# Attention stage of a graph kernel: scores ahead of the keys, and queries between the two gate products, in TensorE's order

## The reference

```python
q = (node_attr @ Wq).reshape(n, H, DQ // H)
x_src = node_attr[src]
# for keys and for values, each with its own weights:
#   rad = relu(edge_attr @ W1 + b1) @ W2 ; g = edge_sh @ Wang.T
#   conv = x_src * g @ Wlin * rad
alpha = jnp.einsum('ehq,qk,ehk->eh', q[dst], Wdot, k)
amax = jax.ops.segment_max(alpha, dst, num_segments=n)
ealpha = jnp.exp(alpha - amax[dst])
denom = jax.ops.segment_sum(ealpha, dst, num_segments=n)
out = jax.ops.segment_sum((ealpha / denom[dst])[..., None] * v, dst, num_segments=n) @ Wout
```

## Time and profile before

| | |
|---|---|
| median of 3 timed runs | 4299.57 us (4296.43 to 4299.69) |
| span of the profiled execution | 5039.6 us |
| TensorE matmuls busy | 4108.6 us, 82% |
| VectorE busy | 3024.4 us, 60% |
| ScalarE busy | 1972.1 us, 39% |
| GpSimd busy | 1919.0 us, 38% |

### The profile page before, as it was taken

The page is one execution under the profiler, slowest core; times in us unless marked ns, Lnnn a source line. Parts: engine busy times, 40 slices in busy tenths (PEclk is TensorE's granted clock), DMA queues, the critical chain, the costliest instruction groups (busy, mean ns, idle before and its releaser), DMA issues. The chain is left out here.

```text
span 5039.6 us, 74127 instructions
## 1 busy us (share of the span) xinstructions
PE 4108.6 (82%) x26543; PEld 3350.2 (66%) x26543; DVE 3024.4 (60%) x4129; ACT 1972.1 (39%) x2885; POOL 1919.0 (38%) x2002
## 2 busy tenths in 40 slices
PE   4667999999999984688888888888888888888832
PEld 4656999999999973465665666666666566666622
DVE  8985544544444342566666666666666666666734
ACT  5754666655665531222222223222223222222313
POOL 5640000000000015555555555555555555555352
PEclk9878999999999985799989999999999999999965
DMA  7998999999998533455555665556666655566433
GB/s 169 188 188 263 298 295 297 294 295 297 292 292 267 182 101 94 133 163 163 164 156 152 166 163 161 162 165 166 164 163 164 166 164 157 159 164 164 141 114 47
DMA packets 1012838, 944.08 MB, mean 187 GB/s; under 512 B 705677, under 2 KB 811929, under 8 KB 1012339
## 3 DMA queue, kind: packets, MB, share of 16 engines
q1 hardware_dynamic: 952099, 814.71, 55.7%
q0 software_dynamic: 60368, 124.52, 11.1%
HBM read 648.66 MB, written 289.97 MB: 186 GB/s over the span
## 5 line engine op out<-in xcount | busy, mean ns | idle before, releaser
L2313 POOL DMA_INDIRECT feats_hops<-x_table,src_s x1616 | 1546.9, 957 | 1223.1 <-PE e_turn_ps L2423 771.8
L1286 PE MATMUL acc<-t_wide,scaled 128*128 128x448 f32 x6860 | 1409.0, 366 | 24.2 <-DVE t_wide L1380 24.2
L1286 PEld LDWEIGHTS acc<-t_wide,scaled 128*128 128x128 f32 x6860 | 1284.3, 188 | 129.2 <-DVE scaled L1398 24.6
L1321 ACT CAST t_wide<-t_ring 128x1568 fp32r<-128x1568 uint8 x490 | 737.7, 1506 | 564.9 <-PE acc L1286 543.8
L1380 DVE CAST t_wide<-t_ring 128x1568 fp32r<-128x1568 uint8 x490 | 478.3, 976 | 733.4 <-PE acc L1286 714.9
L2484 ACT COPY e_out_rows<-e_turn_ps 128x512 f32<-128x512 f32 x404 | 222.1, 588 | 1026.5 <-remote 932.5
L1809 POOL MEMSET l_eps<- 128x1 f32 x1 | 0.1, 104 | 1452.9 <-POOLq L1498 1452.9
L2423 PE MATMUL e_turn_ps<-ident,feats_hops 128*128 128x128 f32 x1616 | 250.3, 296 | 355.6 <-ACT e_out_rows L2484 292.4
L2401 PE MATMUL e_ring_ps<-e_wlin_v,e_x_gv 128*128 128x128 f32 x3232 | 432.7, 281 | 96.9 <-issue 85.6
L2401 PEld LDWEIGHTS e_ring_ps<-e_wlin_v,e_x_gv 128*128 128x128 f32 x3232 | 393.0, 194 | 115.9 <-issue 102.2
L2569 DVE TENSOR_TENSOR e_lw<-e_ring_ps,e_w_t 128x1024 f32<-128x1024 f32 x202 | 247.1, 1223 | 366.9 <-remote 249.6
(11 more groups left out here) (272 smaller groups left out, 5096.2 us busy)
## 6 DMA issues: line engine op xcount, KB each, us to landing
t_ring<-adjacency_bytes SPq DMA_DIRECT2D x490, 512.0 KB, 5.8
sums_table<-e_out_rows SPq DMA_DIRECT2D x202, 576.0 KB
q_first<-hop_zeros_q SPq DMA_DIRECT2D x101, 512.0 KB, 5.9
e_sh<-parts_sh SPq DMA_DIRECT2D x404, 128.0 KB
e_ea<-parts_ea SPq DMA_DIRECT2D x404, 128.0 KB
e_q_rows<-q_first SPq DMA_DIRECT2D x404, 128.0 KB
e_same<-same_row SPq DMA_DIRECT2D x404, 128.0 KB
adjacency_bytes<-lists_staged SPq DMA_DIRECT2D x196, 256.0 KB
```

The source lines that it names most:

```text
L1286: mm = nc.tensor.matmul(acc[c][:, 0:n], U[p][:, b, :], wide[m % WIDE_RING][:, lo:lo + n], start=(b == 0 and p == 0), stop=(b == NB - 1 and ...
L1321: nc.scalar.copy(into, of).then_inc(wide_act, 1)
L2313: nc.gpsimd.indirect_dma_start(x_rows[i % XR][:, g * GT + t, :], None, x1_table, bass.IndirectOffsetOnAxis(ap=src_ix[:, at:at + 1], axis=0 ...
```

## The change

In each turn, TensorE does the scores of the preceding pair in front of `keys_and_radial`, no longer behind it, and the transposes of the queries between gate 0 and gate 1, no longer behind gate 1. Everything else stays.

```diff
@@ -2461,15 +2461,15 @@
                     radial_values(i, j)
                 if chain_at(i - 2) is not None:
                     turn_weights(chain_at(i - 2), i)
+                if on(i - 1):
+                    scores(i - 1)
                 if on(i):
                     keys_and_radial(i)
-                if on(i - 1):
-                    scores(i - 1)
                 if on(i + 1):
                     hidden(i + 1, i)
                     gates(i + 1, 0, p_gk)
+                    turn_q(i + 1)
                     gates(i + 1, 1, p_gv)
-                    turn_q(i + 1)
                 if on(j):
                     spread_out(j, i)
```

## The result

The changed kernel takes 4320.01 us (median of 4 runs, 4319.65 to 4322.35) against 4299.63; the ratio is 1.0048, 95% interval 1.0036 to 1.0061, so 15 to 26 us slower. Five more runs in later rounds gave 4320.91 us, 1.0050 (1.0036 to 1.0063). Forecast were 4327, slower.

The account below looks back on a forecast made before the run. TensorE was taken to set the attention stage's turn. 255 more shape switches at 0.17 us add 43 us, waits won take off 16: +27, put at 4327 us; range 4284 to 4358, the forecast's own 4312 to 4343.

Parts of the forecast that it names:

- The stall: Attention stage: ScalarE's unnamed waits before copying out sums belong to the profiled execution alone, making its missing 740 us.
- TensorE sets the turn: Attention stage: TensorE sets the pace at 10.4 us a turn, ahead of GpSimd's 10.1 and VectorE's 9.4.
- The price of a switch: TensorE's order: each change of array shape costs 0.17 us (0.13 to 0.22); 255 more of them, 43 us.
- The wait won: Second gate's wait for VectorE's key product, every fourth turn: 0.49 less 0.17 before the values, 16 us in 50 groups.
- The sum: Whole kernel: 43 us of switches less 16 us of waits won, +27 us, put at 4327.
- The cheap switches: Rival on TensorE's order: switches below 0.06 us, so the kernel is faster, 4284 or 4275 us; chance 0.17.
- GpSimd as the pace: Rival: GpSimd's 10.1 us or the unnamed stall sets the turn, so time stays the same, 4300 us; chance 0.15.
- no wait is won: Rival at the second gate: no wait goes, so slower still, 4343 to 4365 us; chance 0.1.

Follow-up runs that it names:

- more_switches: Kernel before with scores moved between the hidden matmuls and the gates, and queries between the two gates: 4341.51 us, ratio 1.0098.
- b0_again: The kernel before, unchanged, run once more with a profile: 4297.73 us, ratio 0.9998, profiled span 4296.0.
- scores_between: Kernel before with scores moved between the radial key matmul and the keys, and queries between the gates: 4289.65 us, ratio 0.9979.
- scores_only: Kernel before with only the scores moved in front of the radial key matmul, queries left behind the second gate: 4344.51 us, ratio 1.0104.
- queries_only: Kernel before with only the queries moved between the two gates, scores left behind the keys: 4277.81 us, ratio 0.9949; again 4276.33, 0.9946.
- fewer_switches: Kernel before with order keys, scores, radial key, queries between the gates, and VectorE's two products swapping operands: 4280.03 us, ratio 0.9952.

## Why the prediction was right

*The stall.* Taken for a thing of the one execution because its size was that of the missing 740 us: shown, by a second execution without it. What caused it stays open. That all 740 us lay in the attention stage was not so: 710 did, and the stage has 2133 us without it, where the prediction had 2103.

*TensorE sets the turn.* Right: in `more_switches` two more switches lengthen every kind of turn by 0.31 to 0.37 us (medians, against the queries alone), and TensorE is busy 98% of the stage. But the agreement on which the prediction rested, 10.4 us from the pieces and 10.4 us left for a turn, was in part luck. Its 10.22 us for an ordinary turn are 0.17 too long: it read the values (1.88) in a turn that began behind a wait, and the radial values at 1.19, where `b0_again` has 1.79 and 1.09. It left the wait of every fourth turn (0.53) out of that sum, and its stage was 30 us too short. One kind of turn is set by VectorE: the one with the sum of weights, as long as TensorE's queue isn't longer still. In `scores_between` that turn is 10.34 us (3017.96 to 3028.30 below) and in the change 10.34 too, with one switch more.

```profile
3017.96 2.05 PE L2403 MATMUL e_ring_ps<-e_wlin_v,e_x_gv 128*128 128x128 f32 x16
...
3028.30 1.95 PE L2403 MATMUL e_ring_ps<-e_wlin_v,e_x_gv 128*128 128x128 f32 x16
```

*The price of a switch.* Forecast 0.17; the ordinary turn has +0.16 with one, the turning of weights +0.35 with two (median; +0.39 in the group shown), and 402 of them cost 0.16 each. In its pieces, in the ordinary turn: 0.10 on the keys (0.91 to 1.01), which now end their shape, and 0.05 on the scores (0.53 to 0.58), which now begin it, so that their load isn't ahead. In the turn with weights there are also 0.10 on the radial key, whose load isn't ahead any more, and 0.09 on the last pair of the turning, which now ends its shape.

*The wait won.* Forecast: 0.49 us in the turn with the sum before, 0.17 in front of the values after, 0.32 won in each of 50 groups, 16 us. Measured by the group shown: 0.53 (10.58 less 10.05) before; after it 0.05 in the search turn (10.26 less 10.21) and 0.13 in the turn with the sum (10.34 less 10.21). So 0.35 won, 17 us. The forecast had the place right as well: the 0.05 are the gap in front of the values, and 0.10 of the 0.13 lie in the values themselves, whose first load could not run ahead behind the wait (2.05 us instead of 1.95, load and matmul both at 3035.77, just behind VectorE's gate product that ends at 3035.71):

```profile
3034.50 1.21 DVE L2546 TENSOR_TENSOR feats_hops<-e_ring_ps,e_x_t 128x1024 f32<-128x1024 f32 x1
...
3035.77 1.86 PEld L2401 LDWEIGHTS e_ring_ps<-e_wlin_v,e_x_gv 128*128 128x128 f32 x16
```

The other 0.03 lie at the second gate, where the forecast had none.

*The sum.* +27 forecast, +20.4 measured (15 to 26 by the interval). For a group of four the forecast is 5 switches of 0.17 less 0.32, +0.53 us; the medians of the traces give +0.46 (0.83 less 0.37), 23 us. So the switches were put 1 us too high in all and the wait won 2 us too low, and the timed runs lie 2 to 3 us closer together than these medians say; no single step is shown to be far off. The experiments cut the same sum differently, and the two ways must not be mixed: the queries alone win 21 us, the late keys give 12 back, and the switches on top of that add 30. They are 30 and not 41 (255 by 0.16) because the one in each turn with the sum is covered by VectorE, 8 us.

*The rivals.* The cheap switches fell with `scores_only` and `more_switches`. GpSimd as the pace fell with its 73.6 us of waits for TensorE, and because the added switches show in full. That no wait is won fell with `queries_only`, though the view of waits had shown 4.6 us against the 13.0 of `b0_again`; probably TensorE's own stall covered the wait in that execution, which no run shows.

The rule of the Trainium skill, TensorEngine Tiling (Array Packing), section Tiling Modes, that a changed mode drains TensorE, agrees with these traces: the keys take 1.01 us where they end their shape and 0.91 where they don't. The runs add the price.

## What to carry to other kernels

Where the matrix engine sets the pace, count the changes of the array's shape (rows and columns in use) in its order, and put pieces of one shape side by side; a piece moved for the sake of a wait pays up to two switches in every turn. Test the two halves of a reordering each alone: here one won 21 us and the other lost more. And ask of each kind of turn which engine sets it, for a saving counts only in those in which its engine does. Before a reading of one turn is added up, look whether it began behind a wait.

## What the runs showed of the hardware

A switch of shape costs TensorE about 0.16 us in this fp32 kernel (64 us for 402 of them). The piece in front of it is 0.10 us longer, and the piece behind it longer by a weight load that starts with its matmul and not ahead of it: 0.05 us where the new shape is 128*64 (scores 0.53 to 0.58), 0.10 where it is 128*128 (radial key 0.95 to 1.05). 64 rows straight to 64 columns costs as one switch, not two (radial values into keys in `fewer_switches`, the turn 0.20 us shorter). After a wait the first load isn't ahead either (0.10 us on the values). And a profiled execution can be 17% longer than the timed ones through stalls that the next profile of the same program hasn't got; the timed median is what tells.
